# Expert stage: the gates of each expert pair are spread over its rows by transfers from a turned copy in SBUF, where a matmul and a PSUM copy did it

## The chip, the cores and the metric

The kernel runs on one core of one Trainium2 chip. The metric is the time of one execution on the device in microseconds (us), as the median of several runs.

## What is computed

A small vision tower: Haar wavelet tokens, a linear attention, a mixture of experts, an L1-distance attention and a routed MLP, each with a residual. The change lies in the mixture of experts, whose input is the layer-normed token stream of 8192 tokens by 64 features:

```
logits = x @ gate_w + gate_b                      # 16 experts
top-2 of the logits, softmax over the two         # a gate per token and expert, 14 of 16 are zero
for each expert e:
    hid_e = silu(x @ w1[e]) * (x @ w2[e])         # 64 -> 128
    y_e   = hid_e @ w3[e]                         # 128 -> 64
out = sum over e of gate[:, e] * y_e              # added to h
```

All 16 experts are computed densely for every token; the gate, zero or not, weighs the result.

## The kernel before

There is no scheduler: each engine has its own instruction list, written out by hand, and waits on semaphores (`pe.wait_ge(C["hid"], ...)`). The order of the work is the order of the calls in each engine's part.

The expert stage takes the tokens in 16 groups of 512 (`G4`), and each group in eight steps, k = 0 to 7, of two experts each (e = 0, 1). Features and hidden units lie on the partitions, tokens along the free dimension. In a step:

- TensorE (`moe_group`) makes for each of the two experts two f16 matmuls for w1 (L657, L658: high and low half of the weights, into bank `ps[e]`) and two for w2 (L661, L662, into `ps[2 + e]`). Then it spreads the gates (`moe_spread`, L628), and then does the down projection of the step before (`moe_down`, L636: two experts, each on 64 of the 128 output partitions of bank 4 or 5). L661 of a step waits for `hid` of the same e of the step before, since each bank has one buffer.
- ScalarE takes the silu of `ps[e]` (L1008) and copies the spread gates from bank 7 to the SBUF tile `gB` (L1012).
- VectorE makes `hid` = `ps[2 + e]` times silu (L1392, once per e), then in `weigh` (L1376) the product of the previous step's down projection with `gB`: into `yw`, or for k = 0 into `acc`.
- GpSimd adds `yw` to `acc` (L1538).

Between these lies the work for the next group. In step 0 TensorE turns the next 512 tokens (`moe_turn`, L602), ScalarE copies them (L992, L994) and VectorE makes the low half (L1304). In step 2 TensorE makes the gate logits (`moe_gate`, L608) and the final sum of the group before (`moe_sum`, L646). In steps 3 to 7 VectorE runs the top-2 selection on tiles of 64 elements per partition (`gating`, L1324 to L1354), a few operations behind each `hid`. Its result is `disp`, 128 tokens by 4 by 16 experts. At the end of step 7 TensorE turns `disp` (`moe_weights`, L618, four transposes into bank 7), ScalarE writes the high f16 half of the turned gates to `gT` (L999) and VectorE the low half (`low_weights`, L1361). `gT` then has one row per expert, high in rows 0 to 15 and low in rows 32 to 47, and the matmul of L628 with the constant `both` (ones in the right rows) spreads two of these rows over 64 partitions each.

The SyncE queue issues no transfer between the weight loads at the start and the end of the expert stage; then it feeds the L1 attention (`fill_blocks`, L435).

Of the kernel before, what the change touches and what calls it, by code (L numbers as in the profile page):

```python
# [12 lines left out]
F32 = mybir.dt.float32  # L13
# [6 lines left out]
P = 128  # L20
# [54 lines left out]
def constants():  # L75
    ops = wavelet_operators()
    rows = np.zeros((2, 64, 4, 2, 8))
    for b in range(2):
        rows[b, :, :, b, :] = ops.transpose(2, 0, 1)
    cols = np.zeros((7, 2, 8, 2, 64))  # L80
    for m, (row, col) in enumerate(MAPS):
        cols[m, row % 2, :, row // 2] = ops[col]


    pick = np.zeros((4, 32, 8, 4, 32))
    for g in range(8):
# [7 lines left out]
    both = np.zeros((2, 32, 8, 2, 64))
    for e in range(EXPERTS):
        both[0, e, e // 2, e % 2] = 1.0
        both[1, e, e // 2, e % 2] = 1.0 / LO_SCALE
    same_head = np.kron(np.eye(16), np.ones((8, 8)))
    rank = np.broadcast_to(EXPERTS - np.arange(EXPERTS), (P, EXPERTS))
    return {  # L100
        "c_rows": rows.reshape(P, 64).astype(np.float32),
        "c_cols": cols.reshape(7, 2 * 8 * P).astype(np.float32),
        "c_pick": pick.reshape(P, 8 * P).astype(np.float16),
        "c_both": both.reshape(64, 8 * P).astype(np.float16),
        "c_head": same_head.astype(np.float32),
        "c_ident": np.eye(P, dtype=np.float32),
        "c_rank": np.ascontiguousarray(rank).astype(np.float32),
    }


def build(nc, a, out, scratch):

    with ExitStack() as ctx:
# [3 lines left out]
        def sem(name):  # L117
# [50 lines left out]
        gst = sb("gst", [P, 7, 4])  # L168
        disp = sb("disp", [P, 2, 4, EXPERTS])
        both = sb("both", [64, 8, P], F16)  # L170
        gT = sb("gT", [64, 512], F16)
        eye2 = sb("eye2", [P, D])
# [3 lines left out]
        silu = absd0[:, 2048:3072].rearrange("p (a n) -> p a n", a=2)  # L176
        gB = absd0[:, 3072:4096].rearrange("p (a n) -> p a n", a=2)
        acc = absd0[:, 4096:5120].rearrange("p (a n) -> p a n", a=2)
# [13 lines left out]
        kexp = [t[:, 0:512].rearrange("p (a b) -> p a b", a=8) for t in early]  # L192
        qv = [t[:, 512:1536].rearrange("p (u a m) -> p u a m", u=4, a=2) for t in early]
        score = sb("score", [P, 2, 2, 256])
        attn = sb("attn", [P, S + 1, HEADS])
# [65 lines left out]
            "xs", "xT_ps", "xT_sb", "xh", "xl", "logit_ps", "logit_sb", "gate", "gap", "tanh", "disp",  # L261
            "gT_ps", "gT", "gb_ps", "gb", "h1_ps", "h2_ps", "silu", "hid", "y_ps", "yw", "acc", "fin_ps", "sum", "eye2")}

# [94 lines left out]
        ATTN_IN = 16 * 18  # L358
        MOE_IN = 16 * 6
        L1_IN = 16 * 5  # L360
        GATE = 14
        MLP_IN = 16 * 6
        PADS = 19

# [3 lines left out]
        def _(sp):  # L368
# [32 lines left out]
            sp.dma_start(rank[:], a["c_rank"]).then_inc(moe_in, 16)  # L401
            sp.dma_start(both[:].rearrange("p a b -> p (a b)"), a["c_both"]).then_inc(moe_in, 16)
            sp.dma_start(pick[:].rearrange("p a b -> p (a b)"), a["c_pick"]).then_inc(moe_in, 16)
# [75 lines left out]
        def _(pe):  # L479
# [134 lines left out]
            def moe_weights(g, b):  # L614
                pe.wait_ge(C["disp"], 3 * g + 3)
                pe.wait_ge(C["gb"], 8 * g)
                for j in range(4):
                    mm = pe.transpose(ps[7][0:16, P * j:P * j + P], disp[:, b, j, :], ident[:])  # L618
                mm.then_inc(C["gT_ps"], 1)

            def moe_spread(g, k):
                if k == 0:
                    pe.wait_ge(C["gT"], 2 * g + 2)
                elif k == 3:
                    pe.wait_ge(C["gate"], GATE * (g + 1) + 1)
                else:
                    pe.wait_ge(C["gb"], 8 * g + k)
                pe.matmul(ps[7], both[:, k, :], gT[:], start=True, stop=True).then_inc(C["gb_ps"], 1)  # L628

# [19 lines left out]
            def moe_group(g, b, first, second=False):  # L649
                pe.wait_ge(C["xh"], g + 1)  # L650
                pe.wait_ge(C["xl"], g + 1)
                for k in range(8):
                    n = 8 * g + k
                    for e in range(2):
# [7 lines left out]
                        pe.matmul(ps[2 + e], w12_lo[:, 1, 2 * k + e, :], x2[:, b, :], start=False, stop=True).then_inc(C["h2_ps"], 1)  # L662
                    moe_spread(g, k)
                    if not (first and k == 0):
# [5 lines left out]
                    if k == 2:  # L670
                        pe.wait_ge(C["gb"], 8 * g + 3)
                        moe_gate(g + 1)
                        if not first:
                            moe_sum(g - 1, 1 - b, g + 2)
# [16 lines left out]
            pe.wait_ge(C["sum"], G4)  # L691
            pe.wait_ge(C["gT"], 2 * G4 + 2)

# [234 lines left out]
        def _(act):  # L928
# [66 lines left out]

            def moe_weights(g):
                act.wait_ge(C["gT_ps"], g + 1)
                act.wait_ge(C["gb_ps"], 8 * g)
                nc.scalar.activation(gT[0:16, :], ps[7][0:16, :], ACT.Copy, scale=1.0 / LO_SCALE).then_inc(C["gT"], 1)  # L999

            def moe_group(g, b, first):
                for k in range(8):
                    n = 8 * g + k
                    for e in range(2):
                        act.wait_ge(C["h1_ps"], 2 * n + e + 1)
                        if not (first and k == 0):
                            act.wait_ge(C["hid"], 2 * n + e - 1)
                        nc.scalar.activation(silu[:, e, :], ps[e], ACT.Silu, scale=1.0 / W_SCALE).then_inc(C["silu"], 1)  # L1008
                    act.wait_ge(C["gb_ps"], n + 1)
                    if not (first and k < 2):  # L1010
                        act.wait_ge(C["yw"], n - 1)
                    nc.scalar.copy(gB[:, k % 2, :], ps[7]).then_inc(C["gb"], 1)  # L1012
                    if k == 0:
                        moe_x(g + 1, 1 - b)
                    if k == 5:
                        act.wait_ge(C["gap"], g + 2)
                        nc.scalar.activation(gst[:, 5, :], gst[:, 4, :], ACT.Tanh, scale=0.5).then_inc(C["tanh"], 1)
                    if k == 7:
                        moe_weights(g + 1)
# [4 lines left out]
            moe_weights(0)  # L1024
            for b in range(2):
# [171 lines left out]
        def _(dve):  # L1197
            dve.memset(kT[:], 0.0)
            dve.memset(attn[:, S, :], 0.0).then_inc(pads, 1)
            dve.memset(gT[:], 0.0).then_inc(pads, 1)  # L1200
            dve.memset(osb[:], 0.0).then_inc(pads, 1)
# [3 lines left out]
            for t in (xT4[D:KA, :], xT1[D:KA], xTq[D:KA, :], yT[D:KA, :], gate[D:KA, :], wqv[D:KA, :], fan[D:KA, :], wi[D:KA, :], xT5[D:KA]):  # L1205
                dve.memset(t, 0.0).then_inc(pads, 1)
            dve.wait_ge(pads, 14)
            for t in (xT4[D:D + 1, :], xT1[D:D + 1], xTq[D:D + 1, :], yT[D:D + 1, :], xT5[D:D + 1]):
# [97 lines left out]
            def gating(g, b):  # L1306
# [46 lines left out]
                dve.wait_ge(C["disp"], 3 * g + 2)  # L1353
                dve.tensor_scalar(disp[:, b, :, :], one, 0.5 * LO_SCALE, None, ALU.mult).then_inc(C["disp"], 1)  # L1354
                assert n[0] == GATE
                yield

            def low_weights(g):

                dve.wait_ge(C["gT"], 2 * g + 1)  # L1360
                dve.scalar_tensor_tensor(out=gT[32:48, :], in0=gT[0:16, :], scalar=-LO_SCALE, in1=ps[7][0:16, :],  # L1361
                                         op0=ALU.mult, op1=ALU.add).then_inc(C["gT"], 1)

            def weigh(g, b, k, at):
                dve.wait_ge(C["y_ps"], 8 * g + k + 1)
                dve.wait_ge(C["gb"], 8 * g + k + 1)
                if k == 0:

                    if at >= 2:
                        dve.wait_ge(C["fin_ps"], g - 1)  # L1370
                    out = acc[:, b, :]
                else:
                    if not (at == 0 and k < 3):
                        dve.wait_ge(C["acc"], 7 * g + k - 2 if k > 2 else 7 * g)
                    out = yw[:, k % 2, :]
                dve.tensor_tensor(out, ps[4 + k % 2], gB[:, k % 2, :], ALU.mult).then_inc(C["yw"], 1)  # L1376

# [5 lines left out]
            def moe_group(g, b, last, at):  # L1383
                gates = None
                for k in range(8):
# [19 lines left out]
                    if k == 7:  # L1405
                        for _ in gates:
                            pass
                        low_weights(g + 1)

            low_x(0, 0)  # L1410
            for _ in gating(0, 0):
                pass
            low_weights(0)
            for b in range(2):
# [227 lines left out]
```

## Time and profile before

| | |
|---|---|
| median of 3 runs | 2579.07 us (2578.93 to 2579.52) |
| profiled execution, its own time | 2576.05 us |
| its span, first to last instruction | 2574.2 us |
| TensorE busy | 2236.6 us, 87% |
| VectorE busy | 2244.8 us, 87% |
| ScalarE busy | 1475.2 us, 57% |
| GpSimd busy | 1767.2 us, 69% |

The profile is one execution. It names each instruction by engine, source line, output and input tile, with the idle time ahead of it and what ended that. The tiles `hid`, `silu`, `gB` and `acc` lie in one big tile and appear as `absd`; `x2` appears as `x`, all PSUM banks as `pp`. In the timelines a matmul is drawn with its latency, so consecutive matmuls overlap; the distance between two starts is what a matmul costs TensorE.

### The profile page before, as it was taken

To read this page: it belongs to the slowest core of one execution; us is meant where nothing else is said; L and a number is where in the kernel's file an instruction comes from. 1 tells how busy PE (TensorE), PEld (TensorE's weight loads), DVE (VectorE), ACT (ScalarE), POOL (GpSimd) and SP (SyncE) were. 2 spreads that over 40 slices of the span, in tenths; PEclk is the share of its full clock that TensorE was granted. 3 is DMA by queue.
4 is the path that set the end of the run, shared out by engine and by line. 5 is a ranking of instruction groups with operands and counts; after the bars stand their busy time and mean duration, and the time that the engine had idled before them with its cause. 6 is when DMAs were issued, how large, how long until landed. Compare 5 with 4: busy or idle time off the path is not lost.

```text
span 2574.2 us, 45353 instructions
## 1 busy us (share of the span) xinstructions
PE 2236.6 (87%) x12251; PEld 961.1 (37%) x12251; DVE 2244.8 (87%) x2638; ACT 1475.2 (57%) x3772; POOL 1767.2 (69%) x1033
## 2 busy tenths in 40 slices
PE   5558999999388989989989989899899899899878
PEld 3443333333123333333333333333333333333347
DVE  3877777777879999999999999999999999999974
ACT  0325555555146666666666666666666666666656
POOL 0112333333459889888888988888898888889843
PEclk8788999999689999999999999999999999999979
DMA  5200000000012112121211221221221212212201
GB/s 132 65 1 1 1 0 0 0 0 0 3 47 52 48 48 52 48 50 49 51 48 48 52 50 45 51 51 45 50 52 48 50 48 50 50 47 52 50 19 32
DMA packets 163216, 102.06 MB, mean 40 GB/s; under 512 B 55773, under 2 KB 161182, under 8 KB 163039
## 3 DMA queue, kind: packets, MB, share of 16 engines
q1 hardware_dynamic: 162858, 101.41, 16.0%
q8 instruction: 21, 0.34, 0.1%
q10 hardware_dynamic: 316, 0.12, 0.0%
q14 instruction: 21, 0.17, 0.0%
HBM read 10.63 MB, written 4.19 MB: 6 GB/s over the span
## 4 chain that ended last, share of the span: by engine, by line
PE 65%; DVE 23%; issue 9%; ACT 1%; DMA 1%; DVEq 0%; SPq 0%; POOL 0%; ACTq 0%; POOLq 0%
DVE score L1454 17%; PE pp L802 16%; PE pp L796 7%; PE pp L636 5%; PE pp L767 3%; PE pp L657 3%; PE pp L723 3%; PE pp L715 2%; PE pp L661 2%; PE pp L731 2%; PE pp L711 2%; PE pp L721 2%; PE pp L658 2%; PE pp L662 2%; PE pp L628 2%
## 5 line engine op out<-in xcount | busy, mean ns | idle before, releaser
L1454 DVE TENSOR_REDUCE score<-pp 128x16 f32<-128x1024 f32 x1408 | 1647.0, 1219 | 101.9 <-PE pp L802 82.2
L1571 POOL TENSOR_TENSOR absd<-absd 128x2560 f32<-128x2560 f32 x635 | 1442.4, 2271 | 197.1 <-ACT absd L1074 157.2
L802 PE MATMUL pp<-blocks,pick 128*128 128x512 f16 x2816 | 817.0, 383 | 155.0 <-DVE score L1454 150.4
L1074 ACT ACTIVATE absd<-pp 128x512 f32<-128x512 f32 x1280 | 695.4, 598 | 368.0 <-PE pp L796 364.1
L802 PEld LDWEIGHTS pp<-blocks,pick 128*128 128x128 f16 x2816 | 211.2, 98 | 590.7 <-DVE score L1454 421.9
L796 PE MATMUL pp<-blocks,pick 128*128 128x512 f16 x1280 | 400.0, 383 | 2.1
L1538 POOL TENSOR_TENSOR absd<-absd,yw 128x512 f32<-128x512 f32 x112 | 142.1, 1269 | 318.8 <-DVE yw L1376 318.8
L1008 ACT ACTIVATE absd<-pp 128x512 f32<-128x512 f32 x256 | 150.7, 596 | 148.1 <-PE pp L658 146.6
L1392 DVE SCALAR_TENSOR_TENSOR absd<-pp,absd 128x512 f32<-128x512 f32 x256 | 172.5, 688 | 52.9 <-ACT absd L1008 38.4
L796 PEld LDWEIGHTS pp<-blocks,pick 128*128 128x128 f16 x1280 | 119.8, 97 | 248.3 <-ACT absd L1074 84.6
L1056 ACT CAST qk<-pp 128x512 f16<-128x512 f32 x130 | 76.0, 585 | 191.2 <-PE pp L724 191.2
L1086 ACT ACTIVATE expd<-attn 128x65 f32<-128x65 f32 x512 | 157.5, 329 | 2.7 <-DMA attn<-score 2.7
L636 PE MATMUL pp<-absd 128*64 128x512 f32 x512 | 138.1, 618 | 0.0
L1086 ACT ACTIVATION_READ_ACCUMULATOR expd<-attn 128x1 f32 x512 | 107.6, 210 | 0.0
L657 PE MATMUL pp<-x,absd 128*128 128x512 f16 x256 | 98.4, 384 | 0.6
L661 PE MATMUL pp<-x,absd 128*128 128x512 f16 x256 | 97.8, 382 | 0.3
L658 PE MATMUL pp<-x,absd 128*128 128x512 f16 x256 | 97.5, 381 | 0.0
L662 PE MATMUL pp<-x,absd 128*128 128x512 f16 x256 | 97.4, 380 | 0.0
L1376 DVE TENSOR_TENSOR yw<-pp,absd 128x512 f32<-128x512 f32 x112 | 77.2, 689 | 17.7 <-PE pp L636 15.3
L1012 ACT COPY absd<-pp 128x512 f32<-128x512 f32 x128 | 74.9, 585 | 27.6 <-PE pp L628 18.7
L767 PEld LDWEIGHTS pp<-vb,attk 64*64 64x64 f32 x2048 | 70.7, 136 | 52.9 <-issue 52.6
L767 PE MATMUL pp<-vb,attk 64*64 64x64 f32 x2048 | 88.1, 226 | 0.0
(227 smaller groups left out, 2497.9 us busy)
## 6 DMA issues: line engine op xcount, KB each, us to landing
blocks<-qk SPq DMA_DIRECT2D x1032, 64.0 KB, 2.0
attn<-score SPq DMA_DIRECT2D x1024, 16.0 KB, 1.8
xs<-xn SPq DMA_DIRECT2D x66, 32.0 KB, 1.8
big<-in_wrb_t SPq DMA_DIRECT2D x1, 2064.0 KB
big<-in_x_rows SPq DMA_DIRECT2D x4, 512.0 KB, 6.1
token_rows<-big SPq DMA_DIRECT2D x8, 256.0 KB, 2.0
big<-in_L_ffn_w SPq DMA_DIRECT2D x4, 512.0 KB, 10.1
out<-h SPq DMA_DIRECT2D x16, 128.0 KB, 2.0
```

Of the source, the lines that this page charges most:

```text
L636: mm = pe.matmul(ps[4 + k % 2][64 * e:64 * e + 64, :], w3[:, 2 * k + e, :], hid[:, 2 * (k % 2) + e, :], start=True, stop=True)
L657: pe.matmul(ps[e], w12_hi[:, 0, 2 * k + e, :], x2[:, b, :], start=True, stop=False)
L661: pe.matmul(ps[2 + e], w12_hi[:, 1, 2 * k + e, :], x2[:, b, :], start=True, stop=False)
L767: mm = pe.matmul(ps[7][at, P:P + D], attk[at, n, :], vb[at, odd, n, :], start=False, stop=(n == HEADS - 1))
L796: pe.matmul(ps[4 + n], pick[:, unit % 8, :], blocks[:, b, unit // 16, unit // 8 % 2, :], start=True, stop=True).then_inc(X["diffA"], 1)
L802: mm = pe.matmul(ps[bank + n], pick[:, unit % 8 + n, :], blocks[:, b, unit // 16, unit // 8 % 2, :], start=True, stop=True)
L1008: nc.scalar.activation(silu[:, e, :], ps[e], ACT.Silu, scale=1.0 / W_SCALE).then_inc(C["silu"], 1)
L1074: nc.scalar.activation(absd[odd][:, 16 * u + 8 * n:16 * u + 8 * n + 8, :], ps[4 + n].rearrange("p (h w) -> p h w", w=D), ACT.Abs).then_inc ...
L1086: op = nc.scalar.activation(expd[:, n, :], attn[:, :, n], ACT.Exp, scale=-(float(D) ** -0.5), accum_out=zst[:, 0, n:n + 1])
L1392: dve.scalar_tensor_tensor(out=hid[:, 2 * (k % 2) + e, :], in0=ps[2 + e], scalar=1.0 / W_SCALE, in1=silu[:, e, :], op0=ALU.mult, op1=ALU.m ...
L1454: dve.tensor_reduce(score[:, odd, b, 16 * d:16 * d + 16], pp[:, bank:bank + 2, :].rearrange("p n (h w) -> p (n h) w", w=D), AX.X, ALU.add, ...
L1571: nc.gpsimd.tensor_tensor(x[:, :, 0:w], x[:, :, 0:w], x[:, :, w:2 * w], ALU.add).then_inc(X["tree"], 1)
```

## The change

The matmul that spreads the gates, the ScalarE copy behind it, the constant `both`, and the split of the gates into a high and a low half are gone. VectorE now writes `disp` with each gate eight times ([128, 4, 8, 16]; 512 elements a partition where it were 64). The four transposes then give 128 rows, expert e in the rows e, e + 16, ..., e + 112. ScalarE copies all of bank 7 in f32 to `gT`, which has two buffers. The SyncE queue makes two transfers per step, one per expert: each reads the eight rows of its expert, eight times each, and writes 64 partitions by 2 KB of `gB`. `gB` has four buffers now, with a semaphore each, and lies in the tile `blocks` of the later L1 attention. A transfer waits for the `weigh` of four steps before, and `weigh` for its two transfers.

```
-        disp = sb("disp", [P, 2, 4, EXPERTS])
-        both = sb("both", [64, 8, P], F16)
-        gT = sb("gT", [64, 512], F16)
+        disp = sb("disp", [P, 2, 4, 8, EXPERTS])
+        gT = sb("gT", [P, 2, 512])
...
-        gB = absd0[:, 3072:4096].rearrange("p (a n) -> p a n", a=2)
...
+        gB = blocks[:].rearrange("p a b c n -> p (a b c n)").bitcast(F32).rearrange("p (a n) -> p a n", a=4)
...
+            def spread_gates(g, b, first):
+
+                sp.wait_ge(C["gT"], g + 1)
+                for k in range(8):
+                    if not (first and k < 4):
+                        sp.wait_ge(C["yw"], 8 * g + k - 3)
+                    for e in range(2):
+                        row = 2 * k + e
+                        sp.dma_start(gB[64 * e:64 * e + 64, k % 4, :],
+                                     gT[row:P:EXPERTS, b, :].unsqueeze(1).to_broadcast([8, 8, 512])).then_inc(C[f"gb{k % 4}"], 16)
+
+            for b in range(2):
+                spread_gates(b, b, b == 0)
+            with sp.Fori(1, G4 // 2) as i:
+                for b in range(2):
+                    spread_gates(2 * i + b, b, False)
...
             def moe_weights(g, b):
                 pe.wait_ge(C["disp"], 3 * g + 3)
-                pe.wait_ge(C["gb"], 8 * g)
                 for j in range(4):
-                    mm = pe.transpose(ps[7][0:16, P * j:P * j + P], disp[:, b, j, :], ident[:])
+                    mm = pe.transpose(ps[7][:, P * j:P * j + P], disp[:, b, j, :, :].rearrange("p c e -> p (c e)"), ident[:])
                 mm.then_inc(C["gT_ps"], 1)
-
-            def moe_spread(g, k):
-                if k == 0:
-                    pe.wait_ge(C["gT"], 2 * g + 2)
-                elif k == 3:
-                    pe.wait_ge(C["gate"], GATE * (g + 1) + 1)
-                else:
-                    pe.wait_ge(C["gb"], 8 * g + k)
-                pe.matmul(ps[7], both[:, k, :], gT[:], start=True, stop=True).then_inc(C["gb_ps"], 1)
...
-                    moe_spread(g, k)
...
-            def moe_weights(g):
+            def moe_weights(g, b, at):
                 act.wait_ge(C["gT_ps"], g + 1)
-                act.wait_ge(C["gb_ps"], 8 * g)
-                nc.scalar.activation(gT[0:16, :], ps[7][0:16, :], ACT.Copy, scale=1.0 / LO_SCALE).then_inc(C["gT"], 1)
+                if at >= 1:
+
+                    act.wait_ge(C["yw"], 8 * (g - 1))
+                nc.scalar.copy(gT[:, b, :], ps[7]).then_inc(C["gT"], 1)
...
-                    act.wait_ge(C["gb_ps"], n + 1)
-                    if not (first and k < 2):
-                        act.wait_ge(C["yw"], n - 1)
-                    nc.scalar.copy(gB[:, k % 2, :], ps[7]).then_inc(C["gb"], 1)
...
-                dve.tensor_scalar(disp[:, b, :, :], one, 0.5 * LO_SCALE, None, ALU.mult).then_inc(C["disp"], 1)
+                dve.tensor_scalar(disp[:, b], one.unsqueeze(2).to_broadcast([P, 4, 8, EXPERTS]), 0.5, None, ALU.mult).then_inc(C["disp"], 1)
...
-            def low_weights(g):
-
-                dve.wait_ge(C["gT"], 2 * g + 1)
-                dve.scalar_tensor_tensor(out=gT[32:48, :], in0=gT[0:16, :], scalar=-LO_SCALE, in1=ps[7][0:16, :],
-                                         op0=ALU.mult, op1=ALU.add).then_inc(C["gT"], 1)
-
             def weigh(g, b, k, at):
                 dve.wait_ge(C["y_ps"], 8 * g + k + 1)
-                dve.wait_ge(C["gb"], 8 * g + k + 1)
+                dve.wait_ge(C[f"gb{k % 4}"], 32 * (2 * g + k // 4 + 1))
...
-                dve.tensor_tensor(out, ps[4 + k % 2], gB[:, k % 2, :], ALU.mult).then_inc(C["yw"], 1)
+                dve.tensor_tensor(out, ps[4 + k % 2], gB[:, k % 4, :], ALU.mult).then_inc(C["yw"], 1)
...
-                        low_weights(g + 1)
```

On TensorE, at the end of a group (steps 6 and 7 and the turn of the gates), this stood before; L657 to L662 are w1 and w2, L628 the spreading, L636 the down projection, L618 the turn:

```order
L661 MATMUL pp<-x,absd 128x512
L662 MATMUL pp<-x,absd 128x512
L628 MATMUL pp<-gT,both 128x512
L636 MATMUL pp<-absd 64x512 x2
L618 MATMUL pp<-ident,disp 16x128 x4
L657 MATMUL pp<-x,absd 128x512
L658 MATMUL pp<-x,absd 128x512
```

And this stands there now (the turn is L627):

```order
L661 MATMUL pp<-x,absd 128x512
L662 MATMUL pp<-x,absd 128x512
L636 MATMUL pp<-absd 64x512 x2
L627 MATMUL pp<-ident,disp 128x128 x4
L657 MATMUL pp<-x,absd 128x512
L658 MATMUL pp<-x,absd 128x512
```

The down projection follows the last w2 matmul directly, and each transpose gives 128 rows where it gave 16.

On VectorE, from the end of the gating in step 6 to the first `hid` of the next group, this stood before (L1392 is `hid`, L1376 `weigh`, L1361 `low_weights`):

```order
L1354 TENSOR_SCALAR disp<-gsc 128x64
L1374 REGISTER_ALU
L1376 TENSOR_TENSOR yw<-pp,absd 128x512
L1388 ISA
L1392 SCALAR_TENSOR_TENSOR absd<-pp,absd 128x512
L1388 REGISTER_ALU
L1392 SCALAR_TENSOR_TENSOR absd<-pp,absd 128x512
L1374 REGISTER_ALU
L1376 TENSOR_TENSOR yw<-pp,absd 128x512
L1360 ISA
L1361 SCALAR_TENSOR_TENSOR gT<-gT,pp 16x512
L1388 ISA
```

And now (`hid` is L1382, `weigh` L1366):

```order
L1350 TENSOR_SCALAR disp<-gsc 128x512
L1364 REGISTER_ALU
L1366 TENSOR_TENSOR yw<-pp,blocks 128x512
L1378 ISA
L1382 SCALAR_TENSOR_TENSOR absd<-pp,absd 128x512
L1378 REGISTER_ALU
L1382 SCALAR_TENSOR_TENSOR absd<-pp,absd 128x512
L1364 REGISTER_ALU
L1366 TENSOR_TENSOR yw<-pp,blocks 128x512
L1378 ISA
```

The write of `disp` has eight times the elements, and the 512-element operation of `low_weights` is gone; the rest of the order is as it was.

## Rows read from the trace of the kernel before

**Rows 1.** The head of the page.
```profile
span 2574.2 us, 45353 instructions
```

**Rows 2.** Busy time by stretch: expert stage, L1 attention, weight loads.
```profile
core 0: us, PE busy (x) PEld busy (x) DVE busy (x) ACT busy (x) POOL busy (x), PEclk, DMA share, GB/s
450.00:500.00 50.00, 49.83 (x220) 17.27 (x220) 40.34 (x80) 28.54 (x52) 17.18 (x15) 1.00 0.00 0
1000.00:1100.00 100.00, 90.92 (x526) 37.16 (x524) 95.22 (x91) 63.38 (x174) 89.23 (x51) 1.00 0.20 48
60.00:64.00 4.00, 0.00 (x0) 0.00 (x0) 3.93 (x3) 0.00 (x0) 0.00 (x0) 0.50 1.21 210
```

**Rows 3.** Timeline of TensorE, step 4: start us, us, what.
```profile
448.64 0.39 PE L657 MATMUL pp<-x,absd 128*128 128x512 f16 x1
...
450.16 0.38 PE L662 MATMUL pp<-x,absd 128*128 128x512 f16 x1
450.47 0.39 PE L628 MATMUL pp<-gT,both 64*128 64x512 f16 x1
450.79 1.08 PE L636 MATMUL pp<-absd 128*64 128x512 f32 x4
...
451.80 0.39 PE L657 MATMUL pp<-x,absd 128*128 128x512 f16 x1
```

**Rows 4.** Timeline of TensorE, step 7 and the step behind it.
```profile
459.73 0.10 PEld L661 LDWEIGHTS pp<-x,absd 128*128 128x128 f16 x1 [0.44 <-DVE absd L1392]
...
459.96 0.38 PE L662 MATMUL pp<-x,absd 128*128 128x512 f16 x1
...
460.59 1.08 PE L636 MATMUL pp<-absd 128*64 128x512 f32 x4
...
461.69 0.60 PE L618 MATMUL pp<-ident,disp 128*16 128x128 f32 x4
...
462.13 0.38 PE L657 MATMUL pp<-x,absd 128*128 128x512 f16 x1
...
463.42 0.38 PE L661 MATMUL pp<-x,absd 128*128 128x512 f16 x1
```

**Rows 5.** Timeline of VectorE, steps 3 to 7 of a group.
```profile
446.88 0.69 DVE L1392 SCALAR_TENSOR_TENSOR absd<-pp,absd 128x512 f32<-128x512 f32 x1 [1.65 <-ACT absd L1008]
...
457.50 1.00 DVE L1346 TENSOR_TENSOR gsc<-gsc 128x64 f32<-128x64 f32 x1
...
458.98 0.69 DVE L1392 SCALAR_TENSOR_TENSOR absd<-pp,absd 128x512 f32<-128x512 f32 x1 [0.22 <-DVE gsc L1347]
...
460.10 0.20 DVE L1354 TENSOR_SCALAR disp<-gsc 128x64 f32<-128x64 f32 x1
...
460.88 1.28 DVE L1392 SCALAR_TENSOR_TENSOR absd<-pp,absd 128x512 f32<-128x512 f32 x2
...
463.03 0.68 DVE L1361 SCALAR_TENSOR_TENSOR gT<-gT,pp 16x512 f16<-16x512 f16 x1 [0.28 <-ACT gT L999]
```

**Rows 6.** Timeline of VectorE, the next group's first `hid` of step 3.
```profile
475.31 0.69 DVE L1392 SCALAR_TENSOR_TENSOR absd<-pp,absd 128x512 f32<-128x512 f32 x1 [1.65 <-ACT absd L1008]
```

**Rows 7.** Timelines elsewhere: four 128-by-128 transposes; a one-source VectorE operation of 512.
```profile
106.70 0.60 PE L560 MATMUL pp<-ident,blocks 128*128 128x128 f32 x4
...
703.69 0.41 DVE L1430 TENSOR_SCALAR wqv<-wqv 96x512 f32<-96x512 f32 x1
```

**Rows 8.** Timeline: the copy of the turned gates; the group's first `weigh`.
```profile
462.41 0.59 ACT L999 ACTIVATE gT<-pp 16x512 f16<-16x512 f32 x1 [0.78 <-PE pp L618]
...
469.03 0.69 DVE L1376 TENSOR_TENSOR absd<-pp,absd 128x512 f32<-128x512 f32 x1
```

**Rows 9.** DMA issues: what, count, KB each, median us from issue to landing.
```profile
blocks<-qk SPq DMA_DIRECT2D x1032, 64.0 KB, 2.0
...
token_rows<-big SPq DMA_DIRECT2D x8, 256.0 KB, 2.0
```

**Rows 10.** Timeline of SyncE, L1 attention: eight transfers issued in a row.
```profile
1019.09 5.08 SPq L435 DMA_DIRECT2D blocks<-qk  x8
```

More of the change, by code:

```diff
@@ L92, in constants @@
                 pick[3, y, g, x, y] = -1.0 / LO_SCALE
[L94 to L97, printed above, removed]
     same_head = np.kron(np.eye(16), np.ones((8, 8)))
@@ L103, in constants @@
         "c_pick": pick.reshape(P, 8 * P).astype(np.float16),
-        "c_both": both.reshape(64, 8 * P).astype(np.float16),
         "c_head": same_head.astype(np.float32),
@@ L261, in build @@
             "xs", "xT_ps", "xT_sb", "xh", "xl", "logit_ps", "logit_sb", "gate", "gap", "tanh", "disp",
-            "gT_ps", "gT", "gb_ps", "gb", "h1_ps", "h2_ps", "silu", "hid", "y_ps", "yw", "acc", "fin_ps", "sum", "eye2")}
+            "gT_ps", "gT", "gb0", "gb1", "gb2", "gb3", "h1_ps", "h2_ps", "silu", "hid", "y_ps", "yw", "acc", "fin_ps", "sum", "eye2")}
         l1_in = sem("l1_in")
@@ L358, in build @@
         ATTN_IN = 16 * 18
-        MOE_IN = 16 * 6
+        MOE_IN = 16 * 5
         L1_IN = 16 * 5
@@ L362, in build @@
         MLP_IN = 16 * 6
-        PADS = 19
+        PADS = 18
         w12_f = big2[:, 0:PAIRS * D].rearrange("p (w e n) -> p w e n", w=2, e=EXPERTS)
@@ L401, in _ @@
             sp.dma_start(rank[:], a["c_rank"]).then_inc(moe_in, 16)
-            sp.dma_start(both[:].rearrange("p a b -> p (a b)"), a["c_both"]).then_inc(moe_in, 16)
             sp.dma_start(pick[:].rearrange("p a b -> p (a b)"), a["c_pick"]).then_inc(moe_in, 16)
@@ L670, in moe_group @@
                     if k == 2:
-                        pe.wait_ge(C["gb"], 8 * g + 3)
+                        pe.wait_ge(C["gT"], g + 1)
                         moe_gate(g + 1)
@@ L691, in _ @@
             pe.wait_ge(C["sum"], G4)
-            pe.wait_ge(C["gT"], 2 * G4 + 2)
+            pe.wait_ge(C["gT"], G4 + 1)
             pe.wait_ge(xn_ready[2], 1)
@@ L1018, in moe_group @@
                     if k == 7:
-                        moe_weights(g + 1)
+                        moe_weights(g + 1, 1 - b, 0 if first else 1)
             moe_x(0, 0)
@@ L1023, in _ @@
             nc.scalar.activation(gst[:, 5, :], gst[:, 4, :], ACT.Tanh, scale=0.5).then_inc(C["tanh"], 1)
-            moe_weights(0)
+            moe_weights(0, 0, 0)
             for b in range(2):
@@ L1199, in _ @@
             dve.memset(attn[:, S, :], 0.0).then_inc(pads, 1)
-            dve.memset(gT[:], 0.0).then_inc(pads, 1)
             dve.memset(osb[:], 0.0).then_inc(pads, 1)
@@ L1206, in _ @@
                 dve.memset(t, 0.0).then_inc(pads, 1)
-            dve.wait_ge(pads, 14)
+            dve.wait_ge(pads, 13)
             for t in (xT4[D:D + 1, :], xT1[D:D + 1], xTq[D:D + 1, :], yT[D:D + 1, :], xT5[D:D + 1]):
@@ L1412, in _ @@
                 pass
-            low_weights(0)
             for b in range(2):
```

## The prediction

> **What bounds the kernel now.** The page gives a span of 2574.2 us [rows 1]; the profiled execution took 2576.05 us, 3.0 less than the median of 2579.07. I make the sum against the profiled execution and take the difference off the median, since the 3 us lie outside what changes. I first read busy time by stretch. In the expert stage TensorE is busy 49.83 of 50 us at a granted clock of 1.00, that is at 2.4 GHz, VectorE 40.34, ScalarE 28.54, GpSimd 17.18, and no transfer runs [rows 2]. That says "TensorE bound", but a busy share with drawn latencies can hide short waits, so the timelines of one group come next.
>
> TensorE in step 4: from the first w1 matmul to that of the next step 3.16 us. From the last w2 matmul to the spreading matmul 0.31 us, from there to the down projection 0.32 [rows 3]. So the spreading costs TensorE about 0.315 us per step, and all 128 of them 40.3 us. The step without it would be 2.85.
>
> VectorE in steps 3 to 7 shows why not all of that can be had. Its first `hid` of step 3 starts at 446.88 after an idle time of 1.65, its `hid` of step 6 for e = 1 at 458.98, ending at 459.67 [rows 5]. Between them I find no idle time beyond the 0.22 us that it spends on its own results; `hid`, `weigh` and gating stand back to back. And TensorE waits for it: the weight load of L661 in step 7, at 459.73, comes 0.44 idle behind, released by that `hid` [rows 4]. So **from step 3 to step 7 VectorE already sets the pace** and TensorE is only just behind; from step 7's w2 matmul through step 2 TensorE sets it. The period of a group is 475.31 - 446.88 = 28.43 us [rows 5, 6].
>
> **The change part by part.** I write the times of this group as they would be after the change.
>
> *Steps 3 to 6.* TensorE starts step 3 and VectorE's chain begins behind it as before. The chain has the same operations with the same operands up to the `hid` at 458.98, and none of them waited for a spreading or a copy. TensorE needs 4 x 0.315 = 1.26 us less and waits that much longer for `hid`. Gain: nothing. L661 of step 7 still goes at 459.73.
>
> *Step 7 to step 2 of the next group.* Here TensorE is ahead of nobody and waits for nobody. Four spreadings go: 4 x 0.315 = 1.26 us. In step 7 the down projection started at 460.59 and the turn at 461.69, 1.10 later, where the other steps take 451.80 - 450.79 = 1.01 [rows 3, 4]: the turn waited for ScalarE's last copy out of bank 7, which is gone. That is 0.09 more.
>
> *The turn.* Four transposes with 16 output rows take 0.60 us drawn, 0.44 to the next matmul [rows 4]; four with 128 rows elsewhere 0.60 [rows 7]. Cost nothing.
>
> *The write of* `disp`. 64 elements take 0.20 us [rows 5]. The nearest row for 512 elements from SBUF to SBUF with one source took 0.41 [rows 7]; the dearest of 512 elements here is a two-source 0.69 [rows 5]. I take 0.41, so +0.21, with bounds 0 and +0.49. It lies ahead of the two `hid` of step 7, which run 460.88 to 462.16 [rows 5]. L661 of the next step, e = 1, needs the second one; it went at 463.42 [rows 4] and would now go at 463.42 - 0.315 - 0.09 = 463.02. `hid` is ready by 462.37, at worst 462.65. Covered; without that cover it would cost 0.2 to 0.5 a group. The turn itself would start at 461.28; `disp` is ready at 460.10 + 0.41 = 460.51. Covered too.
>
> *ScalarE.* 128 copies of about 0.6 us go; ScalarE is at 57% here [rows 2] and on no path but the 0.09 above. Copying 128 rows instead of 16 has the same 512 elements per row, so 0.59 as before [rows 8]. *VectorE's* `low_weights`, 0.68 us [rows 5], goes too, between `weigh` and the next `hid`, where VectorE has spare time. Gain nothing.
>
> *The transfers.* SyncE issued eight in 5.08 us [rows 10], 0.64 each; 256 of them are 16 per group, 10.2 us of a period of 27. The queue has nothing else to do in this stage, and a transfer for step k waits for `weigh` of four steps before, which is due three steps before its own use: 8.5 us against two issues and a landing. The tight place is the group's start. The copy of the turned gates began at 462.41 [rows 8] and would now begin near 462.0 and end at 462.6. Two issues bring 463.9. Landing: 64 KB took 2.0 us and 256 KB, also in rows of 2 KB, 2.0 [rows 9]; the new ones have 128 KB. So the gates are there by about 466. The group's first `weigh` was at 469.03 [rows 8] and would be at 469.03 - 0.09 - 3 x 0.315 = 468.0. Behind it VectorE still has its 1.65 us of idle time before the `hid` of step 3 [rows 6], so landing may take 2.0 + 2.0 + 1.65, some 5.6 us, before anything moves. Cost nothing.
>
> *The sum.* Per group 4 x 0.315 = 1.26, by 16 is 20.2; 0.09 by 15 turns is 1.35; the first `disp` of the stage, which TensorE waits for, costs 0.2. **21.4 us**: 2576.05 becomes 2554.7, the median 2557.7. Had the 0.1 us between matmuls on both sides of the spreading not gone with it, one spreading would be 0.215, and the sum 15; that is the lower bound of the term, 2564.
>
> **The rivals.** (a) *TensorE is the bound everywhere.* Then all 128 spreadings count: 40.3 + 1.2 = 41.5, 2537.6. The busy row speaks for it; the wait at L661 in step 7 against it. It would need VectorE's chain to run faster than before, and nothing in the change shortens it.
>
> (b) *TensorE's freed time in steps 0 to 2 is lost as well*, because VectorE, behind its low half of x and its `weigh`, sets the pace there too. Then only step 7 counts: 16 x (0.315 + 0.09) = 6.5, 2572.6. Against it: VectorE idles 1.65 us at the end of this stretch and loses 0.68 us of work in it.
>
> (c) *The transfers become the bound, and the kernel is slower.* A group moves 16 x 128 KB = 2.1 MB. In the L1 attention the engines moved 48 GB/s at a share of 0.20 of 16 engines [rows 2], 15 GB/s per busy engine. All 16 would need 8.7 us per group. But a transfer reads only eight source rows; if that leaves eight engines with work, 120 GB/s and 17.5 us. With the rate of the weight loads, 210 / (16 x 1.21) = 10.8 GB/s [rows 2], 24.2 us, still under 27. If besides reading one row eight times halves the 15 to 7.5, it is 60 GB/s and 34.9 us per group: 6.5 x 16 = 104 us slower, 2683. The point from which it is slower at all is 2.1 MB in 28.7 us, 9.1 GB/s for each of eight engines. The rows in the profile all lie above it.
>
> That eight engines and not 16 do the work is a rule of the Trainium skill ("DMA: Bandwidth & Descriptors", section "Why a DMA increments its semaphore by 16 and not by 1"): the number of engines is the largest up to 16 that divides the slowest dimension of both sides, and here the source's slowest dimension is 8. It speaks against the way this transfer is written. No row here has such a transfer; by that rule alone, with the rates above, the sum stays as it is, and by the one without it as well.
>
> (d) *Only the first gates of a group come late*, since six or eight transfers start in a row and each lands only after 8 us. It eats the gain, 2.4 us over the 5.6 allowed by 15 boundaries is 36 us, less 21 is +15, 2594. Nothing near 8 us with 128 KB is in the profile.
>
> **How the numbers follow.** My sum has 0.70, with its own range 2552 to 2564. (a) 0.09, (b) 0.09, (c) 0.05, (d) 0.03, and 0.04 that something undoes the gain without making it slower. The range 2545 to 2573 takes in the bounds of the spreading's price and (b); it leaves out (a), (c) and (d). A measurement of this kernel can tell 0.2%, 5.2 us, from no change. Faster: 0.70 + 0.09 + 0.09 = 0.88; within 0.2%: 0.04; slower: 0.08.
>
> **What would show it.** In the changed profile: the expert stage's group period is 27.1 us instead of 28.4. TensorE waits longer for `hid` at L661 in steps 5 to 7 (some 1.3 us more per group in all), and the step from 3 to 6 still takes about 3.2 us, while a step 1 takes 2.85. The `weigh` of a group's first step waits for TensorE, not for a transfer, and the transfers land in 2 to 3 us. The L1 attention is unchanged. I am wrong if steps 3 to 6 shrink to 2.85 us (a), if step 1 does not (b), or if `weigh` is released by a transfer (c, d).

## The result, and the profile of the changed kernel

The changed kernel takes 2555.92 us (median of 4 runs, 2554.89 to 2558.59) against 2579.07; the ratio is 0.9912, with a 95% interval of 0.9894 to 0.9929. It is 23.2 us faster, where 21.4 were forecast. Its profiled execution took 2555.99 us with a span of 2554.2.

The head of the changed kernel's page, with busy time and the DMA packets:

```profile
span 2554.2 us, 45035 instructions
## 1 busy us (share of the span) xinstructions
PE 2201.7 (86%) x12123; PEld 951.1 (37%) x12123; DVE 2236.1 (88%) x2620; ACT 1401.1 (55%) x3644; POOL 1764.8 (69%) x1033
...
DMA packets 181569, 135.50 MB, mean 53 GB/s; under 512 B 57805, under 2 KB 163214, under 8 KB 181391
```

ScalarE lost the 74 us of its copies and TensorE 35 us of drawn time; neither number is the gain. The gain shows in the group period. VectorE's first `hid` of step 3 in two groups in a row, from the timeline:

```profile
435.32 0.69 DVE L1382 SCALAR_TENSOR_TENSOR absd<-pp,absd 128x512 f32<-128x512 f32 x1 [1.65 <-ACT absd L1009]
...
447.42 0.69 DVE L1382 SCALAR_TENSOR_TENSOR absd<-pp,absd 128x512 f32<-128x512 f32 x1 [0.22 <-DVE gsc L1343]
...
448.54 0.43 DVE L1350 TENSOR_SCALAR disp<-gsc 128x512 f32<-128x512 f32 x1
...
456.75 0.68 DVE L1366 TENSOR_TENSOR absd<-pp,blocks 128x512 f32<-128x512 f32 x1
...
462.43 0.69 DVE L1382 SCALAR_TENSOR_TENSOR absd<-pp,absd 128x512 f32<-128x512 f32 x1 [1.65 <-ACT absd L1009]
```

The period is 27.11 us, and it is the same within 0.02 in the last twelve of the 15 periods of the stage. Before it was 28.43 in [rows 5, 6], and 28.69 in every second group of the loop. From the first of these `hid` to that of step 6 for e = 1 it is 447.42 - 435.32 = 12.10 us, exactly as before (458.98 - 446.88 in [rows 5]): the chain on VectorE has not moved by a hundredth. TensorE in the same group follows. Step 3 starts with the first line, step 7 with the L657 of 446.43, the next group with that of 450.21 and its step 1 with that of 453.53:

```profile
433.92 0.38 PE L657 MATMUL pp<-x,absd 128*128 128x512 f16 x1
...
443.81 0.38 PE L658 MATMUL pp<-x,absd 128*128 128x512 f16 x1
444.88 0.39 PE L661 MATMUL pp<-x,absd 128*128 128x512 f16 x1 [0.69 <-DVE absd L1382]
445.11 0.38 PE L662 MATMUL pp<-x,absd 128*128 128x512 f16 x1
445.42 1.08 PE L636 MATMUL pp<-absd 128*64 128x512 f32 x4
446.43 0.39 PE L657 MATMUL pp<-x,absd 128*128 128x512 f16 x1
...
448.17 0.39 PE L661 MATMUL pp<-x,absd 128*128 128x512 f16 x1 [0.27 <-DVE absd L1382]
...
449.72 0.66 PE L627 MATMUL pp<-ident,disp 128*128 128x128 f32 x4
...
450.21 0.38 PE L657 MATMUL pp<-x,absd 128*128 128x512 f16 x1
...
453.53 0.38 PE L657 MATMUL pp<-x,absd 128*128 128x512 f16 x1
...
456.36 0.39 PE L657 MATMUL pp<-x,absd 128*128 128x512 f16 x1
```

From the start of step 3 to the second L661 of step 7 it takes 448.17 - 433.92 = 14.25 us, where it took 459.73 - 445.49 = 14.24 before. The four spreadings taken out of it are now waiting in front of L661. Matmuls of this shape follow each other 0.215 us apart where nothing is waited for. In step 6 of the kernel before, the starts of L658 and L661 lay 0.40 us apart:

```profile
456.05 0.38 PE L658 MATMUL pp<-x,absd 128*128 128x512 f16 x1
456.45 0.39 PE L661 MATMUL pp<-x,absd 128*128 128x512 f16 x1
```

That distance was 0.21, 0.40 and 0.33 us in steps 5, 6 and 7, and is 0.49, 1.07 and 0.65 now. These are 1.27 us more, four times 0.315. Step 1 takes 456.36 - 453.53 = 2.83 us, free of its spreading. The last w2 matmul is followed by the down projection after the same 0.31 us that lay between it and the spreading in [rows 3].

The waits of VectorE and TensorE in the expert stage (who waited for whom, us in total, times, longest):

```profile
PEld pp L661 <- DVE absd L1382: 41.4, 62, 1.2
...
PE pp L661 <- DVE absd L1382: 14.0, 31, 0.7
...
DVE yw L1366 <- PE pp L636: 6.0, 29, 0.6
```

No wait for a transfer is among them. From VectorE's first operation of the expert stage to the last group's sum, the stage took 666.75 - 199.94 = 466.8 us before:

```profile
199.94 0.68 DVE L1304 TENSOR_TENSOR x<-pp,x 64x512 f16<-64x512 f32 x1 [2.89 <-ACT x L994]
...
666.75 0.42 DVE L1381 TENSOR_TENSOR h<-pp,h 128x256 f32<-128x256 f32 x1 [2.62 <-PE pp L646]
```

And now 645.06 - 201.24 = 443.8 us:

```profile
201.24 0.69 DVE L1300 TENSOR_TENSOR x<-pp,x 64x512 f16<-64x512 f32 x1 [2.89 <-ACT x L993]
...
645.06 0.42 DVE L1371 TENSOR_TENSOR h<-pp,h 128x256 f32<-128x256 f32 x1 [2.69 <-PE pp L646]
```

So the expert stage gives 23.0 us, which is the gain of the medians. The two spans differ by only 20.0, since in these two executions the work ahead of the stage took 1.3 us longer and the rest behind that sum 1909.1 us instead of 1907.4. In the profiles of experiments 3 and 5, whose code behind the expert stage is the same, the rest is 1910.4 and 1906.7, so I read nothing into these 1.7 us.

The 23.0 us are not 16 equal parts. The two groups ahead of the loop behave otherwise. Their chain on VectorE takes 11.01 us and not 12.10, before as after, so it lets part of TensorE's freed time through: their periods fall from 28.02 and 27.98 us to 26.05 and 26.01, by 1.97 each. The third period falls by 1.12 and the other twelve by 1.45 in the mean, 22.5 us in the 15 periods; the two ends of the stage give the last 0.5.

### The profile page after: what moved, and what is told of

The parts are those of the page before. It is cut to its first block, busy times and chain, and to the rows that moved or that the text cites. A ratio compares the mean times of both kernels' runs of the same rounds, so it can differ in the third digit from the quotient of the medians.

```text
span 2554.2 us, 45035 instructions
## 1 busy us (share of the span) xinstructions
PE 2201.7 (86%) x12123; PEld 951.1 (37%) x12123; DVE 2236.1 (88%) x2620; ACT 1401.1 (55%) x3644; POOL 1764.8 (69%) x1033
## 2 busy tenths in 40 slices
DMA packets 181569, 135.50 MB, mean 53 GB/s; under 512 B 57805, under 2 KB 163214, under 8 KB 181391
## 4 chain that ended last, share of the span: by engine, by line
PE 59%; DVE 27%; issue 10%; ACT 2%; DMA 1%; DVEq 1%; SPq 0%; POOL 0%; ACTq 0%; POOLq 0%
DVE score L1442 17%; PE pp L801 17%; PE pp L795 7%; PE pp L636 4%; PE pp L766 3%; PE pp L722 3%; PE pp L714 2%; PE pp L730 2%; PE pp L710 2%; PE pp L720 2%; DVE absd L1382 2%; PE pp L661 2%; PE pp L657 2%; PE pp L761 2%; PE pp L658 1%
## 5 line engine op out<-in xcount | busy, mean ns | idle before, releaser
L1382 DVE SCALAR_TENSOR_TENSOR absd<-pp,absd 128x512 f32<-128x512 f32 x256 | 173.2, 687 | 54.6 <-ACT absd L1009 40.1
L636 PE MATMUL pp<-absd 128*64 128x512 f32 x512 | 138.1, 618 | 0.4 <-DVE absd L1382 0.4
L661 PE MATMUL pp<-x,absd 128*128 128x512 f16 x256 | 98.0, 383 | 15.5 <-DVE absd L1382 14.0
L657 PE MATMUL pp<-x,absd 128*128 128x512 f16 x256 | 98.4, 384 | 0.0
L662 PE MATMUL pp<-x,absd 128*128 128x512 f16 x256 | 97.5, 381 | 0.0
L658 PE MATMUL pp<-x,absd 128*128 128x512 f16 x256 | 97.5, 381 | 0.0
L1509 POOL TENSOR_TENSOR absd<-absd,qst 128x512 f32<-128x512 f32 x8 | 8.6, 1077 | 116.8 <-DVE qst L1251 106.2
L1366 DVE TENSOR_TENSOR yw<-pp,blocks 128x512 f32<-128x512 f32 x112 | 77.0, 687 | 8.7 <-PE pp L636 6.0
```

The source lines that it names most:

```text
L636: mm = pe.matmul(ps[4 + k % 2][64 * e:64 * e + 64, :], w3[:, 2 * k + e, :], hid[:, 2 * (k % 2) + e, :], start=True, stop=True)
L657: pe.matmul(ps[e], w12_hi[:, 0, 2 * k + e, :], x2[:, b, :], start=True, stop=False)
L661: pe.matmul(ps[2 + e], w12_hi[:, 1, 2 * k + e, :], x2[:, b, :], start=True, stop=False)
L1382: dve.scalar_tensor_tensor(out=hid[:, 2 * (k % 2) + e, :], in0=ps[2 + e], scalar=1.0 / W_SCALE, in1=silu[:, e, :], op0=ALU.mult, op1=ALU.m ...
```

## The experiments

The theory after the result is the prediction's: from step 3 to 7 VectorE's chain sets the pace, elsewhere TensorE; the transfers are hidden. The experiments attack both parts.

**1. Shorten VectorE's chain.** GpSimd's addition starts behind a step's `weigh` and takes 1.27 us, so it runs beside what VectorE does behind the first `hid` of the next step. The operations of the gating keep their order, but the four with two SBUF inputs that stood there, in steps 4 to 6, move behind a second `hid`. In three of these places, ahead of the step's `weigh`, GpSimd adds nothing; in the fourth, in step 6, its addition is nearly over.

```
                 after(dve.tensor_tensor(one, t, wide(r1), ALU.is_equal))
-                yield
                 after(dve.scalar_tensor_tensor(out=two, in0=one, scalar=-1e30, in1=logit[:], op0=ALU.mult, op1=ALU.add))
+                yield
                 after(dve.tensor_reduce(m2, two, AX.X, ALU.max))
...
                 after(dve.tensor_reduce(r2, t, AX.X, ALU.max))
+                yield
                 after(dve.tensor_tensor(two, t, wide(r2), ALU.is_equal))
+                after(dve.tensor_tensor(t, one, two, ALU.subtract))
                 yield
                 yield
                 dve.wait_ge(C["tanh"], g + 1)
-                after(dve.tensor_tensor(t, one, two, ALU.subtract))
                 after(dve.tensor_tensor(t, t, wide(th), ALU.mult))
-                yield
```

> The changed kernel, with the gating's operations on VectorE in the same order but in other places: those with two SBUF inputs stand behind the second hid of a step instead of the first, where GpSimd is done with its addition. Theory (VectorE's chain sets the pace from step 3 to 7): the three operations that took 0.68, 0.76 and 1.00 us instead of 0.22 fall back, the chain gets some 1.6 us shorter per group, TensorE's freed time in steps 3 to 6 (1.3 us, with its old waits 1.55 per group) becomes real: about 24 us faster than the changed kernel, 2532, group period 25.6. Rival (TensorE sets the pace, the period of 27.1 has another cause): no change, 2556.

Measured: 2530.36 us (2528.3 to 2531.45), ratio to the kernel before 0.981 (0.9794 to 0.9827). Three operations of the chain in the changed kernel, and the GpSimd additions beside them, from the timelines of the two engines:

```profile
438.60 1.27 POOL L1526 TENSOR_TENSOR absd<-absd,yw 128x512 f32<-128x512 f32 x1 [4.26 <-DVE yw L1366]
...
442.56 1.27 POOL L1526 TENSOR_TENSOR absd<-absd,yw 128x512 f32<-128x512 f32 x1 [2.35 <-DVE yw L1366]
445.58 1.28 POOL L1526 TENSOR_TENSOR absd<-absd,yw 128x512 f32<-128x512 f32 x1 [1.75 <-DVE yw L1366]
```

```profile
439.27 0.68 DVE L1329 SCALAR_TENSOR_TENSOR gsc<-gsc,logit 128x64 f32<-128x64 f32 x1
...
443.16 0.76 DVE L1337 TENSOR_TENSOR gsc<-gsc,gst 128x64 f32<-128x64 f32 x1
...
445.94 1.00 DVE L1342 TENSOR_TENSOR gsc<-gsc 128x64 f32<-128x64 f32 x1
446.98 0.23 DVE L1343 TENSOR_TENSOR gsc<-gsc,gst 128x64 f32<-128x64 f32 x1
```

Each of the three ends just behind its addition: 439.95 against 439.87, 443.92 against 443.83, 446.94 against 446.86. L1343, behind the third, takes 0.23.

And the same four after the move (now L1328, L1338, L1339 and L1344), with the first `hid` of step 3 ahead of them and of the next group:

```profile
449.39 0.69 DVE L1382 SCALAR_TENSOR_TENSOR absd<-pp,absd 128x512 f32<-128x512 f32 x1 [1.65 <-ACT absd L1009]
...
451.81 0.22 DVE L1328 SCALAR_TENSOR_TENSOR gsc<-gsc,logit 128x64 f32<-128x64 f32 x1
...
457.56 0.21 DVE L1338 TENSOR_TENSOR gsc<-gsc,gst 128x64 f32<-128x64 f32 x1
457.81 0.23 DVE L1339 TENSOR_TENSOR gsc<-gsc 128x64 f32<-128x64 f32 x1
...
460.07 0.40 DVE L1344 TENSOR_TENSOR gsc<-gsc,gst 128x64 f32<-128x64 f32 x1
...
474.91 0.69 DVE L1382 SCALAR_TENSOR_TENSOR absd<-pp,absd 128x512 f32<-128x512 f32 x1 [1.65 <-ACT absd L1009]
```

The chain takes 10.07 us instead of 12.10. The period falls to 25.52 us, and TensorE's freed time of steps 3 to 6 comes in. This version is 48.8 us faster than the kernel before and 25.6 faster than the changed one: the best of this study.

**2. The same move in the kernel before.** The edit is the same.

> The same move in the kernel before. Theory: TensorE still has its spreadings and waited only about 0.3 us per group for VectorE, so it gains 4 to 6 us, about 2574. Rival (the move is worth the same everywhere): 24 us, 2555.

Measured: 2571.16 us (2569.93 to 2572.65), ratio 0.997 (0.9958 to 0.9983), 8 us faster. The period is 28.02 in both kinds of group. That is a third of what the move gives in the changed kernel. So neither is worth its full price alone; the spreading matmul and the chain on VectorE hid each other. Put the other way round: behind the move, the change of this document is worth 2571.16 - 2530.36 = 40.8 us and not 23. That is what rival (a) of the prediction, with TensorE as the bound everywhere, gives for all 128 spreadings (40.3 us).

The theory said 4 to 6. The period of 28.43 falls by 0.41 in the 14 groups of the loop, which is 5.7 us. The rest is that the longer period of every second group, 28.69, is gone as well. The added 0.26 us stood between the turn and the next step's first matmul (0.69 instead of 0.44, below), six times in all, each time where the loop over two groups begins anew. The profile shows nothing that this weight load waited for. Why it is gone here and in the changed kernel I did not test.

```profile
490.12 0.60 PE L618 MATMUL pp<-ident,disp 128*16 128x128 f32 x4
490.81 0.39 PE L657 MATMUL pp<-x,absd 128*128 128x512 f16 x1
```

This is from the timeline of the kernel before, the second group of the pair whose first is in [rows 4].

**3. No transfers.** Only the first group's gates are transferred and waited for; 15 groups are weighed with them.

```
-            for b in range(2):
-                spread_gates(b, b, b == 0)
-            with sp.Fori(1, G4 // 2) as i:
-                for b in range(2):
-                    spread_gates(2 * i + b, b, False)
+            spread_gates(0, 0, True)
...
-                dve.wait_ge(C[f"gb{k % 4}"], 32 * (2 * g + k // 4 + 1))
+                if at == 0:
+                    dve.wait_ge(C[f"gb{k % 4}"], 32 * (2 * g + k // 4 + 1))
```

> The changed kernel with the transfers of the first group alone; the other groups are weighed with the gates of the first and don't wait for transfers (the gates of 15 groups are wrong). Theory: transfers are hidden, 2556 within 1.5 us, same group period 27.1. Rival: their traffic or landing costs time, and it is 3 us or more faster.

Measured: 2555.58 us (2555.21 to 2556.03), the changed kernel's 2555.92 within the scatter. The transfers cost nothing, neither by landing nor by their traffic of 83 GB/s.

**4. Every transfer twice**, the first time into a tile that is unused in this stage.

```
+                    for e in range(2):
+                        row = 2 * k + e
+                        sp.dma_start(spare[64 * e:64 * e + 64, k % 4, :],
+                                     gT[row:P:EXPERTS, b, :].unsqueeze(1).to_broadcast([8, 8, 512])).then_inc(C[f"gb{k % 4}"], 16)
...
-                dve.wait_ge(C[f"gb{k % 4}"], 32 * (2 * g + k // 4 + 1))
+                dve.wait_ge(C[f"gb{k % 4}"], 64 * (2 * g + k // 4 + 1))
```

> The changed kernel with every transfer made twice, the first time into an unused tile, and weigh waits for both. Theory (each transfer runs on eight DMA engines, as the count of small packets says, and these are busy 0.35 x 16 / 8 = 70% of the stage): eight engines would need 140% of the time, the group takes about 38 us, +170 us, 2730. Rival (16 engines share the work): 70% busy and 21 us of issuing in 27, no more than 5 us slower.

Measured: 2742.29 us (two runs, 2742.09 and 2742.5), 186 more than the changed kernel. Busy time and DMA share of the expert stage, first 50 us of the changed kernel, then 200 us of this one, in the columns of [rows 2] (the last three numbers are the granted clock, the DMA share of 16 engines and GB/s):

```profile
450.00:500.00 50.00, 48.14 (x226) 18.30 (x226) 39.84 (x81) 20.83 (x38) 17.13 (x16) 1.00 0.35 83
```

```profile
300.00:500.00 200.00, 150.07 (x622) 48.42 (x622) 113.97 (x235) 58.80 (x105) 47.70 (x43) 0.96 0.47 109
```

The load doubles, but the share stops at 0.47, which is eight of 16 engines nearly full. Its waits now name the transfers:

```profile
DVE yw L1371 <- DMA blocks<-gT: 132.2, 67, 3.4
```

SyncE issues all the time here, 32 transfers a group at a median of 1.2 us, which also makes 38 us. That is no bound of its own: with nothing ahead of it an issue takes 0.6 us in the changed kernel, and in experiment 8, where the engines are slower, the median is 4.6, so its time follows that of the transfers.

So rival (c) of the prediction is real, and the changed kernel is at 0.35 of 0.5, or 70%, of its edge. This agrees with the Trainium skill ("DMA: Bandwidth & Descriptors", "Why a DMA increments its semaphore by 16 and not by 1"), by which the source's slowest dimension of 8 allows eight engines. The packet counts agree as well: the changed kernel has 57805 packets under 512 B where the kernel before had 55773. With 16 added back for the load of `both`, which is gone, this is 2048 more, eight for each of the 256 transfers.

**5. The unread matmul in steps 3 to 6 alone**, in the changed kernel, at the place of the old spreading. It has 512 columns and 128 rows, and writes bank 7 where nobody reads it.

```
+                    if k in (3, 4, 5, 6):
+                        if k < 3:
+                            pe.wait_ge(C["gT"], g + 1)
+                        else:
+                            pe.wait_ge(C["gate"], GATE * (g + 1) + 1)
+                        pe.matmul(ps[7], w12_hi[:, 0, 0, :], x2[:, b, :], start=True, stop=True)
```

> The changed kernel with a matmul of 512 columns that nobody reads put back at the place of the old spreading, in steps 3 to 6 of each group alone. Theory (VectorE's chain sets the pace there): free, 2556, at most 3 us more. Rival (TensorE sets the pace everywhere, the gain was small for another cause): 64 x 0.315 = 20 us slower than the changed kernel, 2576.

Measured: 2554.08 us (2552.85 to 2556.55), the changed kernel's time, and its period of 27.12 in the loop. Sixty-four matmuls are free there, but for the eight of the two groups ahead of the loop, whose periods grow by 0.33.

**6. The same matmul in steps 7, 0, 1 and 2 alone.** The edit has `k in (7, 0, 1, 2)`.

> The same unread matmul in steps 7, 0, 1 and 2 alone. Theory: the whole 64 x 0.315 = 20 us come back, 2576. Rival (VectorE sets the pace here too): 2556 to 2560.

Measured: 2567.49 us (2565.75 to 2571.49), ratio 0.9959 (0.9947 to 0.9972). It costs 11.6 us, so the place is right, but 20 were expected. The timeline says why, here a step 0:

```profile
432.19 0.38 PE L662 MATMUL pp<-x,absd 128*128 128x512 f16 x1
432.40 0.38 PE L668 MATMUL pp<-x,absd 128*128 128x512 f16 x1
432.71 1.08 PE L636 MATMUL pp<-absd 128*64 128x512 f32 x4
```

This matmul starts 0.215 behind its neighbour, the spreading started 0.31 behind [rows 3]. The period is 27.97, 0.86 = 4 x 0.215 over the changed kernel's. For 16 groups that is 13.8 us; the medians say 11.6, and the runs of this kernel lie up to 5.7 us apart.

**7. VectorE's low half gone from the kernel before** (the gates lose their low half).

```
-                    pe.wait_ge(C["gT"], 2 * g + 2)
+                    pe.wait_ge(C["gT"], g + 1)
...
-                        low_weights(g + 1)
```

> The kernel before without VectorE's operation that makes the low half of the turned gates (the gates lose their low half). Theory: VectorE has spare time where it stood, nothing to gain but the wait of the first spreading, 2577 to 2579. Rival (its 16 x 0.68 = 11 us of VectorE time were part of the gain): 2568.

Measured: 2578.14 us (2575.56 to 2580.29), ratio 0.9997 (0.9987 to 1.0006): nothing. The removal of `low_weights` had no part in the gain.

**8. One source row, read 64 times.**

```
-                                     gT[row:P:EXPERTS, b, :].unsqueeze(1).to_broadcast([8, 8, 512])).then_inc(C[f"gb{k % 4}"], 16)
+                                     gT[row:row + 1, b, :].unsqueeze(1).to_broadcast([1, 64, 512])).then_inc(C[f"gb{k % 4}"], 16)
```

> The changed kernel, but each transfer reads one row 64 times instead of eight rows eight times; the slowest dimension of the source is then 64. Theory (the number of engines follows the slowest dimension, and eight copies are there to spread the reading): small packets show 16 engines per transfer instead of 8; if one partition can't feed them, its 128 KB come at one or two engines' rate of 15 GB/s or so, 256 KB per step in 9 to 17 us, and the kernel is 700 us or more slower. Rival (the reads of one row don't hinder each other): 16 engines at 35% busy, faster landing, and the time is the same 2556.

Measured: 3152.42 us (two runs, 3148.69 and 3156.14), 597 more than the changed kernel. Its packets and a stretch of its expert stage:

```profile
DMA packets 183617, 135.50 MB, mean 43 GB/s; under 512 B 59853, under 2 KB 165262, under 8 KB 183439
```

```profile
400.00:800.00 400.00, 236.05 (x752) 67.05 (x752) 135.40 (x271) 70.15 (x124) 57.69 (x50) 0.76 0.87 33
```

The small packets are now 4096 more than in the kernel before, with the 16 added back, so 16 per transfer: all engines take part, and the share is 0.87. VectorE waits for them:

```profile
DVE yw L1366 <- DMA blocks<-gT: 437.9, 88, 8.1
```

They move only 33 GB/s in all, and at that rate the 2.1 MB of a group take 64 us, which is its period. I had put one row at the rate of one or two engines, 15 to 30 GB/s, and the cost at 700 us or more; it holds that one row slows the transfers, but the price was set too high. (The granted clock of 0.76 is that of a TensorE which is busy for 236 of these 400 us.) So this is what the eight copies are for.

**9. As experiment 6, with 64 contraction rows**, as the spreading had: `w12_hi[0:64, 0, 0, :]` and `x2[0:64, b, :]`.

> As the unread matmul in steps 7 to 2, but with 64 contraction rows, as the spreading had, instead of 128; 512 columns as before. There the matmul of 128 rows cost 0.215 us in TensorE's row of starts, the old spreading 0.315. Theory (the change of the number of rows between two matmuls costs the other 0.1): 0.315 each, group period 28.4 instead of 27.97, 6 us more than the run with 128 rows, 2573 to 2575. Rival (the 0.1 was the wait for a semaphore or the signal at its end): 0.215, the same 2567.5.

Measured: 2576.18 us (2572.81 to 2578.72), the period 28.38.

```profile
430.53 0.38 PE L662 MATMUL pp<-x,absd 128*128 128x512 f16 x1
430.84 0.39 PE L668 MATMUL pp<-x,absd 64*128 64x512 f16 x1
431.16 1.08 PE L636 MATMUL pp<-absd 128*64 128x512 f32 x4
```

The 0.31 is back with nothing else changed, so a matmul of 64 rows behind one of 128 starts 0.1 later. Four of them per group cost 28.38 - 27.11 = 1.27 us, which is the prediction's 4 x 0.315. In the medians it is 2576.18 - 2555.92 = 20.3 us, where the prediction had 20.2 for these four.

**10. The moved gating, with the matmul of experiment 5 in steps 3 to 6.**

> The changed kernel with the moved gating operations, and the unread matmul of 128 rows in steps 3 to 6, where it was free before the move. Theory (after the move TensorE sets the pace in these steps): 4 x 0.215 us per group come in, at most 14 us over the 2530.4 of the move alone, 2541 to 2544. Rival (VectorE still sets it): free again, 2530.

Measured: 2542.92 us (2541.88 to 2545.94), 12.6 over the move alone; the period is 26.39, 0.87 over 25.52. The matmul that was free in steps 3 to 6 costs its full 0.215 as soon as the chain on VectorE is shorter. That is the same finding from the other side.

## Why the prediction was right

*What bounds it.* Right, and the decisive step: the busy row said TensorE, the weight load in step 7 released by `hid` said otherwise. Its 0.44 us are not the wait, though. L661 started 0.33 behind L658 there and 0.40 in step 6, against 0.215 without a wait, so TensorE waited 0.30 us a group. Experiments 1, 5, 6 and 10 show the split of the group at step 7.

*Steps 3 to 6, gain nothing.* Right to the hundredth for the groups of the loop: 12.10 us of chain before and after; experiment 5 puts the matmuls back at no cost. In the two groups ahead of the loop part of it was gained, which the prediction, with its 16 equal groups, did not have. Its sign for this part was badly put: it said that steps 3 to 6 would still take about 3.2 us each, and that it is wrong if they shrink to 2.85. They take 2.83, 2.85, 3.13 and 3.70, since the wait gathers in front of the L661 of steps 5 to 7. Only the stretch from step 3 to step 7 as a whole tells, and it is unchanged.

*Step 7 to 2, 1.26 us.* Right: experiment 9 measures 1.27. The split of 0.315 into 0.215 and a gap was left open as a bound; the gap belongs to the 64 rows, and went with the spreading.

*The turn, 0.09 and nothing.* The wait of 0.09 is gone; four 128-row transposes take 449.72 to 450.21, 0.49 and not 0.44, so 0.05 was missed: the 0.60 of [rows 7] is their drawn time, which is not their cost. What was missed the other way is the 0.26 us of every second group, which is absent in the changed kernel; its mean of 0.13 makes the sum 1.26 + 0.09 - 0.05 + 0.13 = 1.43 against 1.45 measured (28.56 - 27.11). The prediction took the period of one group alone. So 21.4 came near 23.2 with two terms left out, this one (six times 0.26, 1.6 us) and the two groups ahead of the loop (0.5 more than the others each). Against them stand the lost 0.05 a group, a dearer start of the stage and a third period that gave 0.3 less.

*The write of* `disp`. 0.43 measured, 0.41 taken, hidden as argued, but for the first one of the stage: from it to the first `hid` it takes 4.23 us instead of 3.91, so 0.3 where 0.2 was taken.

*ScalarE and* `low_weights`, *nothing*. The second is shown by experiment 7. The first was not tried by itself, but experiment 9 leaves little room: it has matmuls like the spreading in steps 7 to 2, where they cost time, and no copies behind them, and its period of 28.38 is within 0.05 of the 28.43 with copies.

*The transfers, nothing.* Right (experiment 3). The group's first `weigh`, at 456.75, waited for no transfer. How soon they land, 2 to 3 us in the prediction, the profile doesn't say. SyncE's eight issues from a group's start took longer than the 0.64 us each that I had taken from the L1 attention, 1.02:

```profile
451.10 8.17 SPq L420 DMA_DIRECT2D blocks<-gT  x8
```

The first three take 0.6 us each, those behind them about 1.2. It costs nothing either, by experiment 3.

*The rivals.* (a) and (b) are excluded by experiments 5 and 6. (a) comes true once VectorE's chain is shorter, as experiments 1 and 2 show. (c) did not come about, but its mechanism is there: eight engines, 83 / (16 x 0.35) = 14.8 GB/s for each busy one, against the 9.1 from which it would decide. Reading a row eight times did not halve the 15 GB/s. (d) did not come about.

## What to carry to other kernels

When two engines are nearly tied, split the period by which one is waited for in each part, and count a removed operation only where its engine sets the pace; then look at what the freed time would need on the other engine, since here a reordering of small operations was worth 8 us alone and 25.6 behind the change. A transfer that replicates rows inside SBUF should be read from several partitions (one instead of eight cost 597 us here), and its load held against the engines that its slowest dimension allows, not against all 16. Look at two periods of an unrolled loop, and at the groups ahead of it, before dividing its time.

## What the runs showed of the hardware that I had not expected

A matmul of 64 contraction rows behind one of 128 starts 0.31 us later where 0.215 is the distance between equals, with the same 512 columns (experiments 6 and 9). The down projection, with 64 output rows in place of 128, also starts 0.31 behind a full one (432.40 to 432.71 in experiment 6). One SBUF row read by all 16 engines gives 33 GB/s (experiment 8), eight rows read by eight engines at least 109 (experiment 4). And three VectorE operations of 64 elements with two SBUF inputs took 0.68, 0.76 and 1.00 us beside GpSimd's addition and about 0.22 away from it. The Trainium skill has this as an exclusive hold on a shared port pair ("SBUF — State Buffer", section "Who interferes with whom"), and the traces agree: in experiment 1 the three fall to 0.22, 0.21 and 0.23. The fourth operation that was moved, 0.23 before, now touches the end of an addition and takes 0.40. In all, 25.6 us go with the move.
